# A post-norm transformer pair on one core: half 1's normed tiles turned one by one, the next batch's norm scales behind its scores, its normed tiles two per step

## The chip, the cores and the metric

The kernel runs on one core of a Trainium2 chip. The metric is the device time of one execution in microseconds; shown are three timed runs and one execution under the profiler. The engines are called TensorE (PE, with PEld for its weight loads), VectorE (DVE), ScalarE (ACT), GpSimd (POOL) and SyncE (SP).

## The reference

8192 tokens of width 256 (8 batches of 1024) go through two layers. Every sublayer adds its input and is normed afterwards. Cut to the part that the last stage computes:

```python
x = _layernorm(x + _L0_attn_ref(...))     # first stage
x = _layernorm(x + _L0_ffn_ref(...))      # experts: second stage; the norm: last stage
...
Q, K, V = X @ W_q + b_q, X @ W_k + b_k, X @ W_v + b_v
A = softmax(einsum('bsd,btd->bst', Q, K) / 16, axis=2)
x = _layernorm(x + einsum('bst,btv->bsv', A, V))
...
scores = sigmoid(xf @ gate.T)              # 8 experts, 2 groups of 4
# the two best of the better group, their scores divided by their sum
lat = xf @ fc1_w.T                         # 256 -> 128
he = relu2(xs @ w1[e].T) @ w2[e].T         # per expert, 128 -> 128
routed = comb @ fc2_w.T                    # 128 -> 256
shared = relu2(xf @ up_w.T) @ down_w.T     # 256 -> 1024 -> 256
x = _layernorm(x + routed + shared)
```

The norm is `(x - mean) / sqrt(var + 1e-5)` over the 256 channels of a token.

## The kernel before, in words

Three stages run one after the other: `stage_a` (first attention and routing), `stage_b` (the first layer's experts) and `stage_c` (everything from the norm in front of the second attention on). Only `stage_c` is touched. It takes one batch of 1024 tokens after the other, as 8 tiles of 128 tokens and, from the third norm on, in two halves of four tiles. Every float32 matrix is kept as a high and a low part, and `product` adds three products (high x high, high x low, low x high).

The order of the work stands in one table, `ORDER`, a list of units; each engine goes through the list and does its share of each unit. The engines meet only through semaphores, so an engine that waits in one unit holds back all its later units. ScalarE takes the batch's loop as a program of its own, with two units placed elsewhere. The units that matter here:

- `("norm3", h)` (L1702): ScalarE norms the four tiles of half `h` of `x2` (memory called `b_wout_raw` in the profile) into `x3` (`b_win_raw`). For half 0 the scales come from VectorE (`ln3`), for half 1 from GpSimd (`scale_second`).
- `("x3T", h)` (L2048 and on): TensorE transposes half `h` of `x3`, two chunks of 128 channels by four tiles, eight transposes (L2053) into two PSUM banks. ScalarE copies the banks as high parts (`c_x3T_hi`), VectorE subtracts for the low parts (`c_x3T_lo`, L1870).
- `("gate", h)`, `("gateT", h)`, `("scoreT", h)`: the router. `route` on VectorE is a chain of small steps; VectorE's copy into `c_scoreT` (L1924) is what SyncE stores and spreads over the partitions.
- `("up", (h, p))`: four products of the shared hidden layer. ScalarE takes the relu (L1738) and the square's high part (L1743), VectorE squares from PSUM (L1957) and so frees the bank, GpSimd subtracts for the low part (a "split", L1567, to `c_place`).
- `("expert", (h, p))`: four experts, each with a product of the latent in one of four PSUM banks and a share of the `down` products, which need the splits of the up units. VectorE multiplies with the scores (L1949) and squares (L1957), ScalarE copies the high part (L1746), GpSimd splits. The bank of expert product `k` is the one that up product `k`, or expert product `k` of the unit before, had: TensorE waits for VectorE's square of it.
- `("latent", h)`, `("comb", h)`, `("out", h)`: latent, combination of the experts, and the sum of everything. For `out`, VectorE adds two banks to `x3` (L1962) and takes four statistics (L1965).
- `("ln2", 0)`: VectorE turns the statistics of the *next* batch's input (`pre`, built up by the `combine` units) into scale and shift for all eight tiles, in the sixteen small steps of `norm_scale` (L148, L149, L150, and L97 through `Chain.then`), each waiting for the one before. `("ln3", 0)` and `("ln4", 0)` run the same sixteen steps on four tiles.
- `norm_x2(b + 1, t)` (L1641, L1630): ScalarE norms tile `t` of the next batch's `pre` into `x2`. It has no unit of its own, but is called inside the expert units: one tile behind each expert's copy, tiles 0 to 3 in `("expert", (0, 1))`, tiles 4 to 7 in `("expert", (1, 0))`. The unit `x2T` at the batch's end transposes them.

The last batch has neither `ln2`, `combine`, `norm_x2` nor `x2T`. The order of the units from half 0's last part on, before:

```python
("combine", 7), ("up", (0, 1)), ("ln2", 0), ("x3T", 1), ("expert", (0, 0)), ("gate", 1), ("expert", (0, 1)), ("gateT", 1),
("comb", 0), ("up", (1, 0)), ("scoreT", 1), ("out", 0), ("latent", 1), ("up", (1, 1)), ("ln4", 0), ("expert", (1, 0)),
("expert", (1, 1)), ("comb", 1), ("x2T", 0), ("x2T", 1), ("out", 1)]
```

Of the kernel before, what the change touches and what calls it, by code (L numbers as in the profile page):

```python
# [33 lines left out]
P = 128  # L34
# [28 lines left out]
def wait_past(eng, sem, value):  # L63

    if not isinstance(value, int) or value > 0:
        eng.wait_ge(sem, value)
# [1228 lines left out]
def stage_c(nc, d, weights, slots, gates, x2, x3_rows, pre, late, results_stored, wqk_raw, wqk_in):  # L1295
# [18 lines left out]
             ("gateT", 0), ("latent", 0), ("mix", 7), ("up", (0, 0)), ("scoreT", 0), ("combine", 6), ("norm3", 1),  # L1314
             ("combine", 7), ("up", (0, 1)), ("ln2", 0), ("x3T", 1), ("expert", (0, 0)), ("gate", 1), ("expert", (0, 1)), ("gateT", 1),
             ("comb", 0), ("up", (1, 0)), ("scoreT", 1), ("out", 0), ("latent", 1), ("up", (1, 1)), ("ln4", 0), ("expert", (1, 0)),
             ("expert", (1, 1)), ("comb", 1), ("x2T", 0), ("x2T", 1), ("out", 1)]
# [30 lines left out]
    with ExitStack() as ctx:  # L1348
# [279 lines left out]
        def _(act):  # L1628
# [12 lines left out]
            def norm_x2(b, t):  # L1641
                if is_first(b) and t % HTILES == 0:
                    act.wait_ge(pre_chain, (t // HTILES + 1) * (HTILES + NORM_STEPS))
                elif t == 0:
                    act.wait_ge(pre_chain, (b + 1) * PRE_STEPS + NORM_STEPS)
                    wait_past(act, x3_done, 2 * b)
                norm = normed(x2, pre, t, pre_scale, pre_shift)
                if t % HTILES == HTILES - 1:
                    norm.then_inc(x2_done, 1)
# [21 lines left out]
            def body(b, end):  # L1671
# [8 lines left out]
                for unit in units:  # L1680
# [16 lines left out]
                    elif kind == "norm3":  # L1697
# [6 lines left out]
                        for t in range(HTILES * j, HTILES * (j + 1)):  # L1704
                            last = normed(x3, x2, t, scale, shift)
                        last.then_inc(x3_done, 1)
                    elif kind == "x3T":
# [17 lines left out]
                    elif kind in ("up", "expert"):  # L1725

                        lag = 1 if kind == "up" else 0
                        for k in range(CHUNKS + lag):
# [18 lines left out]

                            if k < CHUNKS and unit in (("expert", (0, 1)), ("expert", (1, 0))) and not end:
                                norm_x2(b + 1, CHUNKS * j[0] + k)
                            elif k < CHUNKS and unit == ("expert", (1, 1)):  # L1750
                                norm4(b, k)
# [24 lines left out]
        def _(v):  # L1776
# [84 lines left out]
            def body(b, end):  # L1861
# [12 lines left out]
                for unit in order(b):  # L1874
# [83 lines left out]
                    elif kind == "out":  # L1958
                        for g in range(2):
                            at = HTILES * j + 2 * g  # L1960
                            v.wait_ge(v_full, n + g + 1)
                            v.tensor_tensor(x3[:, at:at + 2, :], ps[:, v_bank(unit, g), :].rearrange("p (t c) -> p t c", c=C), x3[:, at:at + 2, :], ALU.add).then_inc(v_free, 1)  # L1962
                        for t in range(HTILES):
                            v.wait_ge(v_free, n + t // 2 + 1)
                            v.bn_stats(stats[:, HTILES * j + t, :], x3[:, HTILES * j + t, :]).then_inc(stats_done, 1)  # L1965
                    elif kind == "ln4":
                        v.wait_ge(x3_done, 2 * b + 2)
                        scale_half(b, 2, 0)
# [33 lines left out]
        def _(pe):  # L2002
# [8 lines left out]
            def body(b, end):  # L2011
# [7 lines left out]
                for unit in order(b):  # L2019
# [28 lines left out]
                    elif kind == "x3T":  # L2048
                        pe.wait_ge(x3_done, 2 * b + j + 1)
                        for c in range(CH):  # L2050
                            out = v_open(pe, b, unit, c)
                            for t in range(HTILES):
                                last = pe.transpose(out[:, bass.ts(t, P)], x3[:, HTILES * j + t, bass.ts(c, P)], ident[:])  # L2053
                            last.then_inc(v_full, 1)
                    elif kind == "gate":
# [144 lines left out]
```

## Time and profile before

| what | us |
|---|---|
| timed runs | 1971.8, 1969.98, 1971.37 |
| their median | 1971.37 |
| the profiled execution | 1963.96 |
| its span | 1961.9 |
| mean granted clock of TensorE | 0.983 |

The span is the time between the first and the last instruction in the profile; the execution's own time is 2.1 us longer. The profiled execution is 0.4% below the median of the timed runs. `stage_c` takes the time from about 722 us on, and from its second batch on one batch follows the other every 151 us (the transposes of half 1 start at 973.64, 1124.98, 1276.20, 1427.42, 1578.35, 1729.42). Batch 1 is the one from which rows are shown. The timeline gives start, duration, engine, line, operation, what is written and read, and in brackets how long the engine was idle before and what released it; instructions of a kind that follow each other stand in one row with their count.

### The profile page before, as it was taken

Reading aid. Unit: us, or ns where it says so; the run is one execution under the profiler, and the core shown is the slowest. Engines: PE = TensorE matmul, PEld = TensorE weight load, DVE = VectorE, ACT = ScalarE, POOL = GpSimd, SP = SyncE. Lnnn points to the kernel's source line nnn. Section 1 sums busy time; section 2 is a strip of 40 time slices with the busy share of each in tenths; the row PEclk is TensorE's granted clock in tenths of the full one; section 3 lists DMA queues with packets and bytes.
Section 4 is the critical chain, followed back from the end, with each engine's and each line's share of the span. In section 5 each row is a group of like instructions: output and inputs, shape, how many; then the busy total and the mean of one; then the engine's idle time right before and its main releaser. Section 6 shows DMA issues by size and latency. Waiting matters only on the chain.

```text
span 1961.9 us, 35538 instructions
## 1 busy us (share of the span) xinstructions
PE 1860.4 (95%) x11756; PEld 1625.0 (83%) x11756; DVE 1354.9 (69%) x3205; ACT 870.6 (44%) x1623; POOL 861.5 (44%) x1165
## 2 busy tenths in 40 slices
PE   7999998599999989999999999999999999999996
PEld 6888887389999978788788788888878878878885
DVE  4788888644444565886886786876876886786664
ACT  4445554333333414444444445345454445444443
POOL 4267778531111142453454354354265265255054
PEclk9999999699999989999999999999999999999998
DMA  4111222323222331112212211221221112111011
GB/s 156 65 65 65 98 75 87 109 93 100 87 86 86 120 82 49 60 44 66 65 44 61 62 53 46 48 82 45 44 84 48 44 45 87 39 49 55 12 44 65
DMA packets 81639, 133.04 MB, mean 68 GB/s; under 512 B 11328, under 2 KB 62144, under 8 KB 81376
## 3 DMA queue, kind: packets, MB, share of 16 engines
q1 hardware_dynamic: 71984, 104.96, 16.0%
q0 software_dynamic: 9520, 26.36, 5.4%
q8 instruction: 75, 1.23, 0.3%
q14 instruction: 60, 0.49, 0.1%
HBM read 105.57 MB, written 25.72 MB: 67 GB/s over the span
## 4 chain that ended last, share of the span: by engine, by line
PE 62%; DVE 6%; issue 5%; POOL 3%; ACT 3%; DMA 1%; POOLq 0%; DVEq 0%; ACTq 0%
PE c_ps L118 10%; PE c_ps L120 10%; PE c_ps L119 10%; PE b_ps L118 5%; PE b_ps L119 5%; PE b_ps L120 5%; PE c_ps L133 3%; PE c_ps L134 3%; PE c_ps L135 3%; PE c_ps L2043 2%; PE c_ps L2104 2%; PE c_ps L2106 2%; PE c_ps L2105 2%; POOL c_pool_tmp L97 1%; ACT b_win_raw L1630 1%
## 5 line engine op out<-in xcount | busy, mean ns | idle before, releaser
L1567 POOL TENSOR_TENSOR c_place<-c_shared_place,c_place 128x512 fp32r<-128x512 f32 x256 | 324.8, 1293 | 197.4 <-ACT c_place L1746 114.3
L1558 POOL DMA_INDIRECT c_gathered<-expert_results,c_slots x112 | 112.2, 1002 | 324.4 <-DVE c_pre L1798 300.9
L1957 DVE SCALAR_TENSOR_TENSOR c_shared_place<-c_ps,c_shared_place 128x512 f32<-128x512 f32 x256 | 170.3, 683 | 54.4 <-ACT c_shared_place L1738 54.2
L118 PE MATMUL c_ps<-c_place 128*128 128x256 f32 (+1 forms) x520 | 149.2, 287 | 10.4 <-DVE c_place L1870 6.4
L1746 ACT ACTIVATE c_place<-c_shared_place 128x512 fp32r<-128x512 f32 x128 | 80.3, 630 | 174.0 <-DVE c_shared_place L1957 173.0
L133 PE MATMUL c_ps<-c_downT_hi,c_place 128*128 128x256 f32 x512 | 151.9, 297 | 2.4 <-POOL c_place L1567 2.4
L119 PE MATMUL c_ps<-c_place 128*128 128x256 f32 (+1 forms) x520 | 147.8, 284 | 0.0
L120 PE MATMUL c_ps<-c_place 128*128 128x256 f32 (+1 forms) x520 | 147.8, 284 | 0.0
L134 PE MATMUL c_ps<-c_downT_lo,c_place 128*128 128x256 f32 x512 | 145.1, 283 | 0.0
L1058 POOL DMA_INDIRECT b_xs<-x_rows,expert_tokens x56 | 57.9, 1033 | 198.3 <-PE b_ps L1246 175.8
L135 PE MATMUL c_ps<-c_downT_hi,c_place 128*128 128x256 f32 x512 | 144.8, 283 | 0.0
L1692 ACT ACTIVATE c_shared_place<-c_ps,c_shift_s 128x1024 f32<-128x1024 f32 x64 | 71.5, 1117 | 160.8 <-DVE c_shift_s L1893 160.2
L118 PE MATMUL b_ps<-b_wout_hi,b_hT_hi 128*128 128x256 f32 x448 | 127.2, 284 | 0.0
L120 PE MATMUL b_ps<-b_wout_hi,b_hT_lo 128*128 128x256 f32 x448 | 126.8, 283 | 0.0
L119 PE MATMUL b_ps<-b_wout_lo,b_hT_hi 128*128 128x256 f32 x448 | 126.7, 283 | 0.0
L118 PEld LDWEIGHTS c_ps<-c_place 128*128 128x128 f32 x520 | 100.4, 193 | 17.9 <-DVE c_place L1870 11.6
L1738 ACT ACTIVATE c_shared_place<-c_ps 128x512 f32<-128x512 f32 x128 | 75.4, 595 | 88.3 <-PE c_ps L120 64.1
L1199 DVE SCALAR_TENSOR_TENSOR b_hT_lo<-b_ps,b_hT_hi 128x512 fp32r<-128x512 f32 x112 | 76.1, 689 | 52.4 <-ACT b_hT_hi L1109 52.4
L118 PE MATMUL c_ps<-c_x3T_hi,c_upT_hi 128*128 128x512 f32 x256 | 100.4, 392 | 5.7 <-DVE c_shared_place L1957 5.7
L133 PEld LDWEIGHTS c_ps<-c_downT_hi,c_place 128*128 128x128 f32 x512 | 97.3, 190 | 9.4 <-POOL c_place L1567 5.4
L118 PE MATMUL c_ps<-c_x2T,c_place 128*128 128x512 f32 x256 | 104.2, 407 | 0.0
L1674 ACT ACTIVATE c_place<-c_ps 128x512 fp32r<-128x512 f32 x128 | 69.2, 594 | 77.2 <-PE c_ps L2043 77.2
(421 smaller groups left out, 6139.6 us busy)
## 6 DMA issues: line engine op xcount, KB each, us to landing
c_x2T<-score_rows SPq DMA_DIRECT2D x64, 512.0 KB, 5.4
b_win_raw<-xT SPq DMA_DIRECT2D x8, 1024.0 KB, 6.5
a_x_rows<-x SPq DMA_DIRECT2D x8, 1024.0 KB, 5.6
x_rows<-a_x SPq DMA_DIRECT2D x8, 1024.0 KB, 4.5
c_pre<-x_rows SPq DMA_DIRECT2D x8, 1024.0 KB, 5.6
out<-b_win_raw SPq DMA_DIRECT2D x16, 512.0 KB, 3.0
b_win_raw<-w_in SPq DMA_DIRECT2D x7, 1024.0 KB, 5.6
b_wout_raw<-w_out SPq DMA_DIRECT2D x7, 1024.0 KB, 6.0
```

Of the source, the lines that this page charges most:

```text
L118: pe.matmul(out, lh, rh, start=(j == 0), stop=False)
L119: pe.matmul(out, lh, rl, start=False, stop=False)
L120: last = pe.matmul(out, ll, rh, start=False, stop=(j == len(terms) - 1))
L133: pe.matmul(out, lh, rh, start=False, stop=False)
L134: pe.matmul(out, lh, rl, start=False, stop=False)
L135: last = pe.matmul(out, ll, rh, start=False, stop=(stop and j == len(terms) - 1))
L1199: v.scalar_tensor_tensor(hT_lo[:, h, k, :], ps[:, bank, :], 0.0, f32(hT_hi[:, h, k, :]), ALU.max, ALU.subtract).then_inc(bank_free, 1)
L1558: pool.indirect_dma_start(rows[:, a, :], None, d["ys"], bass.IndirectOffsetOnAxis(ap=slots[:, a, t:t + 1], axis=0), bounds_check=TRASH + P ...
L1567: pool.tensor_tensor(hid_lo[:, place, :], square[:, place % RING, :], f32(hid_hi[:, place, :]), ALU.subtract).then_inc(hid_split, 1)
L1738: act.activation(relu[:, place % RELU_RING, :], ps[:, s_bank(unit, k), :], ACT.Relu).then_inc(relu_up, 1)
L1746: act.activation(hid_hi[:, place, :], square[:, place % RING, :], ACT.Copy).then_inc(hid_hi_done, 1)
L1957: v.scalar_tensor_tensor(square[:, place % RING, :], ps[:, s_bank(unit, k - lag), :], 0.0, factor, ALU.max, ALU.mult).then_inc(s_free, 1)
```

## The change

It has three parts. (1) `norm3` on ScalarE signals `x3_done` after each tile and no longer once per half; TensorE's `x3T` goes tile by tile, waits for each tile, and turns both chunks of it before the next. The counts that others wait for are adapted (four times as many signals per half). (2) The unit `ln2` moves from its place in front of `("x3T", 1)` to behind `("scoreT", 1)`. (3) `norm_x2` for all eight tiles is called in `("expert", (1, 0))`, two tiles behind each expert's copy.

```diff
-             ("combine", 7), ("up", (0, 1)), ("ln2", 0), ("x3T", 1), ("expert", (0, 0)), ("gate", 1), ("expert", (0, 1)), ("gateT", 1),
-             ("comb", 0), ("up", (1, 0)), ("scoreT", 1), ("out", 0), ("latent", 1), ("up", (1, 1)), ("ln4", 0), ("expert", (1, 0)),
+             ("combine", 7), ("up", (0, 1)), ("x3T", 1), ("expert", (0, 0)), ("gate", 1), ("expert", (0, 1)), ("gateT", 1),
+             ("comb", 0), ("up", (1, 0)), ("scoreT", 1), ("ln2", 0), ("out", 0), ("latent", 1), ("up", (1, 1)), ("ln4", 0), ("expert", (1, 0)),
...
-                    wait_past(act, x3_done, 2 * b)
+                    wait_past(act, x3_done, TILES * b)
...
-                            last = normed(x3, x2, t, scale, shift)
-                        last.then_inc(x3_done, 1)
+                            normed(x3, x2, t, scale, shift).then_inc(x3_done, 1)
...
-                            if k < CHUNKS and unit in (("expert", (0, 1)), ("expert", (1, 0))) and not end:
-                                norm_x2(b + 1, CHUNKS * j[0] + k)
+                            if k < CHUNKS and unit == ("expert", (1, 0)) and not end:
+                                norm_x2(b + 1, 2 * k)
+                                norm_x2(b + 1, 2 * k + 1)
...
-                        v.wait_ge(x3_done, 2 * b + 2)
+                        v.wait_ge(x3_done, TILES * b + TILES)
...
-                        pe.wait_ge(x3_done, 2 * b + j + 1)
-                        for c in range(CH):
-                            out = v_open(pe, b, unit, c)
-                            for t in range(HTILES):
-                                last = pe.transpose(out[:, bass.ts(t, P)], x3[:, HTILES * j + t, bass.ts(c, P)], ident[:])
-                            last.then_inc(v_full, 1)
+                        outs = [v_open(pe, b, unit, c) for c in range(CH)]
+                        for t in range(HTILES):
+                            pe.wait_ge(x3_done, TILES * b + HTILES * j + t + 1)
+                            for c in range(CH):
+                                last = pe.transpose(outs[c][:, bass.ts(t, P)], x3[:, HTILES * j + t, bass.ts(c, P)], ident[:])
+                                if t == HTILES - 1:
+                                    last.then_inc(v_full, 1)
```

On VectorE, at the unit's old place between the squares of up (0, 1) and the low parts of half 1's transposes, before:

```order
L1957 SCALAR_TENSOR_TENSOR c_shared_place<-c_ps,c_shared_place 128x512 x4
L148 TENSOR_TENSOR c_tmp<-c_pre_stats 128x8
L149 TENSOR_TENSOR c_pre_shift<-c_pre_stats 128x8
L150 SCALAR_TENSOR_TENSOR c_tmp<-c_pre_stats 128x8
...
L97 SCALAR_TENSOR_TENSOR c_pre_scale<-c_tmp,c_pre_scale 128x8
L97 SCALAR_TENSOR_TENSOR c_pre_shift<-c_pre_shift,c_pre_scale 128x8
L1870 TENSOR_TENSOR c_x3T_lo<-c_ps,c_x3T_hi 128x512 x2
L1949 SCALAR_TENSOR_TENSOR c_shared_place<-c_ps,c_x2T 128x512 x2
```

In the changed program the low parts (L1870) follow the squares (L1957) at once, and the sixteen steps stand on the same engine behind the copy of half 1's scores:

```order
L1924 COPY c_scoreT<-c_ps 32x128
L148 TENSOR_TENSOR c_tmp<-c_pre_stats 128x8
L149 TENSOR_TENSOR c_pre_shift<-c_pre_stats 128x8
L150 SCALAR_TENSOR_TENSOR c_tmp<-c_pre_stats 128x8
...
L97 SCALAR_TENSOR_TENSOR c_pre_scale<-c_tmp,c_pre_scale 128x8
L97 SCALAR_TENSOR_TENSOR c_pre_shift<-c_pre_shift,c_pre_scale 128x8
L1962 TENSOR_TENSOR b_win_raw<-c_ps,b_win_raw 128x512 x2
L1965 BN_STATS c_stats<-b_win_raw 128x6 x4
L1870 TENSOR_TENSOR c_lat_lo<-c_ps,c_lat_hi 128x512
L1957 SCALAR_TENSOR_TENSOR c_shared_place<-c_ps,c_shared_place 128x512 x4
```

So the sums of half 0 (L1962), its statistics, the latent's low part and the four squares of up (1, 1) now stand behind the sixteen steps.

On TensorE, the transposes of half 1 with what they wait for (line 2053 is `x3T` in both), before and changed:

```order
L2053 MATMUL c_ps<-c_ident,b_win_raw 128x128 [waits c_v_free,c_x3_done]
L2053 MATMUL c_ps<-c_ident,b_win_raw 128x128 x3
L2053 MATMUL c_ps<-c_ident,b_win_raw 128x128 [waits c_v_free]
L2053 MATMUL c_ps<-c_ident,b_win_raw 128x128 x3
L118 MATMUL c_ps<-c_lat_hi,c_w1T_hi 128x512 [waits c_s_free,c_v_free]
```

```order
L2053 MATMUL c_ps<-c_ident,b_win_raw 128x128 [waits c_x3_done,c_v_free]
L2053 MATMUL c_ps<-c_ident,b_win_raw 128x128
L2053 MATMUL c_ps<-c_ident,b_win_raw 128x128 [waits c_x3_done]
L2053 MATMUL c_ps<-c_ident,b_win_raw 128x128
```

The pair with its wait stands four times, once per tile. The product behind it, the first of expert (0, 0), waits for its bank (`c_s_free`) and the latent's low part as before.

## Rows read from the trace of the kernel before

**Rows 1.** The page, part 1: busy time, share of the span, instructions.
```profile
PE 1860.4 (95%) x11756; PEld 1625.0 (83%) x11756; DVE 1354.9 (69%) x3205; ACT 870.6 (44%) x1623; POOL 861.5 (44%) x1165
```

**Rows 2.** Waits: engine, line <- waited for: us in all, times, longest.
```profile
PE c_ps L118 <- DVE c_shared_place L1957: 9.4, 21, 0.9
PE c_ps L2053 <- ACT b_win_raw L1630: 9.3, 7, 1.5
```

**Rows 3.** Timeline, TensorE, batch 1: start, us, instruction [idle before <-releaser].
```profile
973.64 1.09 PE L2053 MATMUL c_ps<-c_ident,b_win_raw 128*128 128x128 f32 x8 [1.50 <-ACT b_win_raw L1630]
974.93 0.47 PE L118 MATMUL c_ps<-c_lat_hi,c_w1T_hi 128*128 128x512 f32 x1 [0.20 <-DVE c_shared_place L1957]
...
976.46 0.39 PE L2093 MATMUL c_ps<-c_zeros 128*128 128x512 bf16 x1 [0.60 <-POOL c_place L1567]
...
981.46 0.39 PE L133 MATMUL c_ps<-c_downT_hi,c_place 128*128 128x256 f32 x1 [0.34 <-POOL c_place L1567]
...
986.31 0.40 PE L120 MATMUL c_ps<-c_x3T_hi,c_gateT_lo 128*8 128x512 f32 x1
987.02 0.47 PE L118 MATMUL c_ps<-c_lat_hi,c_w1T_hi 128*128 128x512 f32 x1 [0.32 <-DVE c_shared_place L1957]
```

**Rows 4.** Timeline, ScalarE, the same stretch.
```profile
971.51 2.07 ACT L1630 ACTIVATE b_win_raw<-b_wout_raw,c_shift,c_scale 128x256 f32<-128x256 f32 x4 [2.24 <-POOL c_shift L97]
973.49 1.05 ACT L1738 ACTIVATE c_shared_place<-c_ps 128x512 f32<-128x512 f32 x2
...
977.78 1.08 ACT L1674 ACTIVATE c_x3T_hi<-c_ps 128x512 fp32r<-128x512 f32 x2
...
997.99 0.17 ACT L1713 ACTIVATE c_expd<-c_ps 128x32 f32<-128x32 f32 x1
```

**Rows 5.** Timeline, VectorE, the same stretch.
```profile
974.10 1.29 DVE L1957 SCALAR_TENSOR_TENSOR c_shared_place<-c_ps,c_shared_place 128x512 f32<-128x512 f32 x2 [2.21 <-ACT c_shared_place L1738]
...
977.48 0.21 DVE L148 TENSOR_TENSOR c_tmp<-c_pre_stats 128x8 f32<-128x8 f32 x1
...
983.79 1.29 DVE L1870 TENSOR_TENSOR c_x3T_lo<-c_ps,c_x3T_hi 128x512 fp32r<-128x512 f32 x2
```

**Rows 6.** Timeline, GpSimd, batch 1: splits for half 0 and for up (1, 0).
```profile
971.43 9.97 POOL L1567 TENSOR_TENSOR c_place<-c_shared_place,c_place 128x512 fp32r<-128x512 f32 x8
...
1006.36 5.10 POOL L1567 TENSOR_TENSOR c_place<-c_shared_place,c_place 128x512 fp32r<-128x512 f32 x4 [7.17 <-DVE c_shared_place L1957]
```

**Rows 7.** Timeline, VectorE, from the sums `out` of half 0 on.
```profile
1009.16 1.27 DVE L1962 TENSOR_TENSOR b_win_raw<-c_ps,b_win_raw 128x512 f32<-128x512 f32 x2
...
1011.67 0.66 DVE L1870 TENSOR_TENSOR c_lat_lo<-c_ps,c_lat_hi 128x512 fp32r<-128x512 f32 x1
...
1017.34 1.27 DVE L148 TENSOR_TENSOR c_tmp<-c_stats 128x4 f32<-128x4 f32 x1
...
1022.48 1.29 DVE L1949 SCALAR_TENSOR_TENSOR c_shared_place<-c_ps,c_x2T 128x512 f32<-128x512 f32 x2
1023.69 0.68 DVE L1957 SCALAR_TENSOR_TENSOR c_shared_place<-c_ps,c_shared_place 128x512 f32<-128x512 f32 x1
```

**Rows 8.** Timeline, VectorE, `ln3` with GpSimd idle: first step, and what follows.
```profile
936.73 0.15 DVE L148 TENSOR_TENSOR c_tmp<-c_stats 128x4 f32<-128x4 f32 x1
...
939.55 1.22 DVE L1889 TENSOR_REDUCE c_neg_max<-c_ps 128x1 f32<-128x1024 f32 x1
```

**Rows 9.** Timeline, TensorE: first products of expert (1, 0) and (1, 1).
```profile
1015.82 0.39 PE L118 MATMUL c_ps<-c_lat_hi,c_w1T_hi 128*128 128x512 f32 x1
...
1024.57 0.41 PE L118 MATMUL c_ps<-c_lat_hi,c_w1T_hi 128*128 128x512 f32 x1
```

**Rows 10.** Windows: stretch: us, TensorE busy (x), granted clock, DMA share, GB/s.
```profile
1124.00:1136.60 12.60, 10.48 (x70) 1.00 0.41 145
...
1275.20:1287.80 12.60, 11.32 (x68) 0.86 0.38 152
...
1278.00:1279.00 1.00, 0.95 (x3) 0.50 0.99 377
```

## The prediction

> **What bounds the kernel now.** I read the page first: TensorE is busy 95% of the span [rows 1]. Work that is moved on another engine therefore counts only where TensorE waits for it. The list of waits shows how little that is in the last stage: 9.3 us for ScalarE's normed tiles and 9.4 us for VectorE's squares, in seven to twenty-one places [rows 2]. Then I took one batch (batch 1, 943 to 1042 us; the batches repeat every 151 us) engine by engine. What the reader is to see there: at the transposes of half 1 TensorE waits 1.50 us, then 0.20 us for VectorE, 0.60 and 0.34 us for GpSimd, then 0.3 us more for VectorE behind the gate product [rows 3], and from there to the next batch it hardly waits. That full stretch is where the sixteen steps of the norm scales (the unit `ln2`) are moved to.
>
> I count 0.2%, some 4 us, as what a measurement of this kernel can tell from no change.
>
> **Half 1's tiles turned one by one.** ScalarE norms four tiles from 971.51 to 973.58, at 0.5 us each, and the eight transposes start at 973.64 [rows 3, 4]. Turned one by one, six of them run earlier and the last two end near 973.9 and not 974.73. But the next product starts at 974.93 because it needs the PSUM bank that VectorE's first square frees (974.10 plus 0.69), and that square needs the relu that ScalarE starts at 973.49, behind the normed tiles [rows 3 to 5]. Nothing in this chain moves. The wait in front of the transposes turns into a longer wait behind them. Nor do copies of the transposes start earlier: ScalarE takes them after the up products' squares. I cost this part at 0; its cover is the relu, and if it were gone GpSimd's first four splits (971.43 plus four at 1.25 us [rows 6]) would still hold TensorE until 976.46. The three added waits on TensorE find their tiles ready in half 0 and fall into idle time in half 1.
>
> **`ln2` leaves its old place.** There the sixteen steps take VectorE from 977.48 to 983.79, 6.31 us [rows 5]. Without them the low part of half 1's transposes, and with it the squares of expert (0, 0), come about 5 us earlier: the copies of ScalarE end at 978.86 [rows 4], so the low parts are done near 979.6 and no longer at 985.0, and the squares follow. What is late next is GpSimd, and it is late already: the products at 976.46 and 981.46 wait for its splits, which run back to back from 971.43 [rows 3, 6], and the change doesn't touch these. So only the third wait goes: the first product of expert (0, 1) starts at 987.02 where it could have followed at 986.31 + 0.23 [rows 3]. **Gain: 0.5 us in each of seven batches** (the eighth has no `ln2`).
>
> **`ln2` in its new place.** VectorE now has it between the copy of half 1's scores and the sums `out` of half 0. All VectorE does for half 1 is queued behind it: the two sums and four statistics, the low part of the latent, the four squares of up (1, 1) and the scales of `ln4`. Two of these have TensorE waiting: the first product of expert (1, 0) needs the latent's low part and the bank that the first of the four squares frees.
> - VectorE comes to this place at 1009.16 [rows 7], with the 0.5 us gained 1008.66.
> - The length of the sixteen steps depends on GpSimd. With GpSimd quiet the same steps on half as many tiles take 2.83 us [rows 8]; `ln4` next to GpSimd's splits takes 5.14 us, its first step alone 1.27 us [rows 7], and `ln2` in its old place 6.31 us. There the last of the eight splits ends at 981.40, twelve steps follow in the 2.4 us until 983.79, 0.2 us each [rows 5, 6], and the first four took the 3.9 us before that: a step that meets a split waits for its end. In the new place the splits of up (1, 0) run until 1011.46 [rows 6], 0.5 us earlier after the change: 2.3 us of being held, with three steps done in it as in `ln4`, then thirteen free ones, 2.6 us. I take 4.9 us.
> - The sums start near 1013.6, the latent's low part 2.51 us later (1009.16 to 1011.67), the first square 0.6 us after that, at 1016.7; it ends at 1017.4, and TensorE follows 0.14 us behind, as at 974.93 [rows 3, 5]. TensorE has been ready since 1015.82 - 0.5 [rows 9]: **it waits 2.2 us, and stands 1.7 us later than before.**
> - The third relu needs the buffer and bank of the first square, so on ScalarE relu, square and relu (some 0.6 us each, as the relus of [rows 4]) follow from 1017.4, then one more square on VectorE, and VectorE comes to `ln4` near 1019.7, not 1017.34: 2.4 us late. `ln4` (5.1 us, since the splits are late too) and the squares up to the first freed bank (1.9 us, 1022.48 to 1024.37 [rows 7]) end near 1026.75. TensorE would be there at 1017.55 + 8.75 + 0.1 = 1026.4 [rows 9]: another 0.5 us of waiting. Before, this bank came only 0.2 us ahead of its use, so there is no slack to take up the delay.
>
> So each batch but the last is **2.3 us longer** at expert (1, 1), all gain counted in. From there to the next batch TensorE is full in both, and the other engines are late by the same amount as TensorE, so they meet it as before.
>
> For the steps' length the Trainium skill (SBUF — State Buffer, Who interferes with whom) has a rule: a VectorE instruction with two SBUF inputs contends with a GpSimd instruction that reads SBUF, and the loser is blocked for the whole of the other's instruction. The trace agrees for the steps named above. By that rule the hold ends with the last split, as I count it; by the plain row of the old place the steps would again take 6.31 us and the batch would be 3.7 us longer.
>
> **The next batch's normed tiles, two per step.** On ScalarE four tiles leave expert (0, 1), where TensorE waits for none, and expert (1, 0) has two per step. One step there is then a copy, some 0.6 us like the others of its size [rows 4], and two tiles of 0.5 us, 1.6 us against the 2.2 us (8.75 over four [rows 9]) that TensorE takes for a step, so ScalarE keeps up. Their reader, the transposes for the next batch, comes a whole expert unit and `comb` later. One side effect is good: ScalarE's exponential for the gate, held by copies and norms until 997.99 [rows 4], can start 1 us earlier, and the routing with it. But the squares behind it follow TensorE's products, so VectorE gains no more than the 0.5 us already counted. No DMA is added or moved: slots, rows and stores are issued behind `out` as before, and half 1's scores go out 0.5 us earlier. Cost 0.
>
> **Sum.** 7 x 2.3 = 16 us. The profiled execution took 1963.96 us (span 1961.9), so its like would be 1980; the timed runs, with their median of 1971.37, are what the forecast is for: **1987.4 us**. Bounds of the one unknown, the steps' length: 2.83 us (GpSimd quiet) brings expert (1, 0) 0.4 us earlier than before, and `ln4` is still 0.2 us late, in all +0.2 us per batch, 1973 us; 6.31 us gives 1014.97 for the sums, +3.7 us per batch, 1997 us. I take the value between because the end of the splits is a row and the hold follows it.
>
> **Rivals.**
> - *It fits (faster).* From 1008.66 to 1015.32 there are 6.66 us, and what must follow the steps takes 3.9 us. If the steps take 2.8 us or less and `ln4` is not late, only the gain remains: 1971.4 - 7 x 0.5 = 1968 us. Against it: the quiet row has 2.83 us, on half as many tiles, and here GpSimd works beside it [rows 6, 8]. Chance 0.08.
> - *Gain and loss even out.* GpSimd's splits, fed earlier, end before VectorE comes. The steps take 3 us: +0.2 to +0.4 us per batch, 1973 to 1974 us. Chance 0.09.
> - *The clock falls behind the new wait.* Once in the trace, after the cluster of waits at batch 3's transposes, the granted clock was 0.50 (1.2 GHz), 0.86 as the mean of the 12.6 us [rows 10], so 3.5 us at half rate; this cost nothing, since TensorE would have waited for GpSimd there. At the new place nothing hides it: 3.5 us at half rate lose 1.75 us per fall. In every batch: 7 x 1.75 = 12, so 2000 us; in two or three, about 1992. For it: the new wait of 2.2 us is longer than any other in the batches. Against: the same cluster of waits in the next earlier batch, 2.6 us in all, left the clock at 1.00 [rows 10]. Chance 0.11.
>
> The forecast keeps 0.72. The range, 1972 to 1998, holds the bounds and most of the clock's case. Faster 0.08, within 0.2% 0.09, slower 0.83.
>
> **What the new profile would show.** Transposes of half 1 in four pairs from 972.1 on and the product behind them still at the same distance from the relu; the wait of the first product of expert (0, 1) gone; the steps of `ln2` behind the scores' copy, 4.9 us long, the first ones ending with a split; a wait of about 2.2 us in front of expert (1, 0) and 0.5 us in front of expert (1, 1), both on VectorE's square; a batch of 153.5 us. I am wrong if the steps take under 3 us, if TensorE doesn't wait there, or if the product after the transposes starts earlier and GpSimd's splits with it.

## The result, and the profile after

| | us |
|---|---|
| changed kernel, median of 4 runs | 1991.21 (1990.76 to 1991.84) |
| kernel before on the same chip, median of 4 runs | 1970.81 (1969.98 to 1971.8) |
| ratio | 1.0103, interval 1.0091 to 1.0115 |
| the changed kernel's profiled execution | 1991.59 |
| its span, and mean granted clock | 1989.5, 0.979 |

The changed kernel is slower by 20.4 us. The profiled executions differ by 27.6 us, which is too much: the one of before started the first expert of `stage_c` at 823.86, the changed one at 830.32, though nothing ahead of `stage_c` was touched (of the eleven further kernels below seven are at 828.8 to 830.7 there, four, all on one other chip, at 824.0 to 827.5). So 6.5 us of the 27.6 come from outside the change, and 21.1 us from the last stage. One of the five timed executions of e2, below, took 3946 us, twice as long as all others, and is left out of its ratio. All below is of that stage, and positions are taken relative to the batch's first product of expert (0, 0).

The page, part 1, of the changed kernel (busy time, share of the span, instructions), to set beside [rows 1]:

```profile
PE 1870.6 (94%) x11756; PEld 1629.9 (82%) x11756; DVE 1352.7 (68%) x3205; ACT 869.3 (44%) x1623; POOL 865.6 (44%) x1165
```

Every engine has as many instructions as before. TensorE shows 10 us more busy time for the same work, part of which is time at the lower clock.

Its list of waits (engine, line <- waited for: us in all, times, longest), as [rows 2]:

```profile
PE c_ps L118 <- DVE c_shared_place L1957: 28.6, 26, 2.0
...
PEld c_ps L2053 <- ACT b_win_raw L1630: 5.7, 21, 0.3
```

The last line is of the transposes' weight loads (PEld), not of their matmuls. Its counterpart before is

```profile
PEld c_ps L2053 <- ACT b_win_raw L1630: 12.5, 8, 1.9
```

The matmuls' own row, 9.3 us before, is no longer in the list: they idle some 0.2 us per batch between the pairs. The weight loads' wait for normed tiles shrank from 12.5 to 5.7 us and fell apart into 21 of at most 0.3 us. The wait for VectorE's squares grew from 9.4 to 28.6 us, of which seven times 2.0 us are new and stand in front of expert (1, 0). It moved, and it grew.

Timeline of TensorE in the changed kernel, batch 1, as [rows 3, 9], and at the end the same two products of batch 5:

```profile
981.76 1.82 PE L2053 MATMUL c_ps<-c_ident,b_win_raw 128*128 128x128 f32 x8
984.44 0.47 PE L118 MATMUL c_ps<-c_lat_hi,c_w1T_hi 128*128 128x512 f32 x1 [0.86 <-DVE c_shared_place L1957]
...
985.98 0.39 PE L2094 MATMUL c_ps<-c_zeros 128*128 128x512 bf16 x1 [0.61 <-POOL c_place L1567]
...
990.96 0.39 PE L133 MATMUL c_ps<-c_downT_hi,c_place 128*128 128x256 f32 x1 [0.35 <-POOL c_place L1567]
...
996.03 0.39 PE L118 MATMUL c_ps<-c_lat_hi,c_w1T_hi 128*128 128x512 f32 x1
...
1026.90 0.47 PE L118 MATMUL c_ps<-c_lat_hi,c_w1T_hi 128*128 128x512 f32 x1 [2.02 <-DVE c_shared_place L1957]
...
1030.55 0.63 PE L118 MATMUL c_ps<-c_lat_hi,c_w1T_hi 128*128 128x512 f32 x1
...
1037.28 0.40 PE L118 MATMUL c_ps<-c_lat_hi,c_w1T_hi 128*128 128x512 f32 x1
...
1644.04 0.47 PE L118 MATMUL c_ps<-c_lat_hi,c_w1T_hi 128*128 128x512 f32 x1 [2.02 <-DVE c_shared_place L1957]
...
1653.59 0.47 PE L118 MATMUL c_ps<-c_lat_hi,c_w1T_hi 128*128 128x512 f32 x1 [0.60 <-DVE c_shared_place L1957]
```

The eight transposes now spread over 1.82 us, and the wait that stood ahead of them stands behind them (0.86). The waits for GpSimd's splits are there as before, 0.61 and 0.35. The wait at expert (0, 1), 996.03, is gone. At 1026.90 stands the new one, 2.02 us. In batch 1 the next product takes 0.63 us where such a one takes 0.40, and expert (1, 1) follows without a second wait (1037.28); in batch 5 the second wait is there, 0.60.

Windows (stretch: us, TensorE busy (x), granted clock, DMA share, GB/s), batch 1 behind the new wait, and batch 5 over the same place:

```profile
1028.00:1031.00 3.00, 3.00 (x15) 0.50 0.11 44
1640.00:1654.00 14.00, 11.38 (x72) 1.00 0.37 132
```

0.50 is the lower level, 1.2 GHz; batch 5 kept 2.4 GHz through.

ScalarE, batch 1, as [rows 4], and the pairs of the next batch's normed tiles:

```profile
981.01 2.08 ACT L1630 ACTIVATE b_win_raw<-b_wout_raw,c_shift,c_scale 128x256 f32<-128x256 f32 x4 [2.25 <-POOL c_shift L97]
983.00 1.06 ACT L1737 ACTIVATE c_shared_place<-c_ps 128x512 f32<-128x512 f32 x2
...
1006.00 0.18 ACT L1712 ACTIVATE c_expd<-c_ps 128x32 f32<-128x32 f32 x1
...
1036.31 0.63 ACT L1745 ACTIVATE c_place<-c_shared_place 128x512 fp32r<-128x512 f32 x1 [6.60 <-DVE c_shared_place L1957]
1036.84 1.08 ACT L1630 ACTIVATE b_wout_raw<-c_pre,c_pre_shift,c_pre_scale 128x256 f32<-128x256 f32 x2
1037.83 0.61 ACT L1745 ACTIVATE c_place<-c_shared_place 128x512 fp32r<-128x512 f32 x1
```

VectorE, batch 1, as [rows 5, 7]:

```profile
983.61 1.29 DVE L1957 SCALAR_TENSOR_TENSOR c_shared_place<-c_ps,c_shared_place 128x512 f32<-128x512 f32 x2 [2.22 <-ACT c_shared_place L1737]
...
987.91 1.29 DVE L1870 TENSOR_TENSOR c_x3T_lo<-c_ps,c_x3T_hi 128x512 fp32r<-128x512 f32 x2 [0.84 <-ACT c_x3T_hi L1674]
...
1018.06 1.08 DVE L148 TENSOR_TENSOR c_tmp<-c_pre_stats 128x8 f32<-128x8 f32 x1
1019.07 0.16 DVE L149 TENSOR_TENSOR c_pre_shift<-c_pre_stats 128x8 f32<-128x8 f32 x1
1019.15 1.26 DVE L150 SCALAR_TENSOR_TENSOR c_tmp<-c_pre_stats 128x8 f32<-128x8 f32 x1
1020.44 0.17 DVE L97 SCALAR_TENSOR_TENSOR c_tmp<-c_tmp 128x8 f32<-128x8 f32 x1
...
1022.97 1.29 DVE L1962 TENSOR_TENSOR b_win_raw<-c_ps,b_win_raw 128x512 f32<-128x512 f32 x2
...
1025.49 0.67 DVE L1870 TENSOR_TENSOR c_lat_lo<-c_ps,c_lat_hi 128x512 fp32r<-128x512 f32 x1
1026.08 1.28 DVE L1957 SCALAR_TENSOR_TENSOR c_shared_place<-c_ps,c_shared_place 128x512 f32<-128x512 f32 x2
...
1029.31 0.17 DVE L148 TENSOR_TENSOR c_tmp<-c_stats 128x4 f32<-128x4 f32 x1
...
1034.38 1.29 DVE L1949 SCALAR_TENSOR_TENSOR c_shared_place<-c_ps,c_x2T 128x512 f32<-128x512 f32 x2
```

GpSimd, batch 1, as [rows 6]:

```profile
980.94 9.97 POOL L1567 TENSOR_TENSOR c_place<-c_shared_place,c_place 128x512 fp32r<-128x512 f32 x8
...
1015.10 5.28 POOL L1567 TENSOR_TENSOR c_place<-c_shared_place,c_place 128x512 fp32r<-128x512 f32 x4 [6.98 <-ACT c_place L1742]
```

The sixteen steps run from 1018.06 to 1022.97: 4.91 us. The first and the third step took 1.08 and 1.26 us, and they end at 1019.14 and 1020.41, 0.03 us behind the ends of the third and the fourth of the splits that run one after the other from 1015.10 to 1020.38. From 1020.44 on the steps come every 0.2 us. Then the sums, the latent's low part at 1025.49, and the square that frees the bank at 1026.08; TensorE follows at 1026.90. `ln4` starts at 1029.31, 44.87 us after the batch's start, where it was 42.41 [rows 7]. Early in the batch VectorE and ScalarE are ahead of where they were: the transposes' low parts start 3.47 us after the batch's first product and not 8.86 (987.91, and [rows 5]), the exponential 21.56 and not 23.06 (1006.00, and [rows 4]). ScalarE's pairs of tiles come every 1.51 us, faster than TensorE's 2.1 us per step.

### The profile page after: what moved, and what is told of

It is laid out like the page before. It is cut to its first block, busy times and chain, and to the rows that moved or that the text cites. A ratio compares the mean times of both kernels' runs of the same rounds, so it can differ in the third digit from the quotient of the medians.

```text
span 1989.5 us, 35538 instructions
## 1 busy us (share of the span) xinstructions
PE 1870.6 (94%) x11756; PEld 1629.9 (82%) x11756; DVE 1352.7 (68%) x3205; ACT 869.3 (44%) x1623; POOL 865.6 (44%) x1165
## 4 chain that ended last, share of the span: by engine, by line
PE 59%; DVE 8%; issue 6%; POOL 4%; ACT 2%; DMA 1%; POOLq 0%; DVEq 0%; ACTq 0%
PE c_ps L118 9%; PE c_ps L120 9%; PE c_ps L119 9%; PE b_ps L118 5%; PE b_ps L120 5%; PE b_ps L119 5%; PE c_ps L133 3%; PE c_ps L135 3%; PE c_ps L134 3%; PE c_ps L2043 2%; POOL c_place L1567 2%; PE c_ps L2105 2%; PE c_ps L2107 1%; PE c_ps L2106 1%; POOL c_pool_tmp L97 1%
## 5 line engine op out<-in xcount | busy, mean ns | idle before, releaser
L1957 DVE SCALAR_TENSOR_TENSOR c_shared_place<-c_ps,c_shared_place 128x512 f32<-128x512 f32 x256 | 170.3, 684 | 49.2 <-ACT c_shared_place L1737 49.0
L133 PE MATMUL c_ps<-c_downT_hi,c_place 128*128 128x256 f32 x512 | 153.8, 300 | 2.1 <-POOL c_place L1567 2.1
L135 PE MATMUL c_ps<-c_downT_hi,c_place 128*128 128x256 f32 x512 | 146.9, 287 | 0.0
L1949 DVE SCALAR_TENSOR_TENSOR c_shared_place<-c_ps,c_x2T 128x512 f32<-128x512 f32 x128 | 86.7, 687 | 52.8 <-PE c_ps L120 42.1
```

Source lines behind the costliest of these rows:

```text
L133: pe.matmul(out, lh, rh, start=False, stop=False)
L135: last = pe.matmul(out, ll, rh, start=False, stop=(stop and j == len(terms) - 1))
L1949: v.scalar_tensor_tensor(square[:, place % RING, :], ps[:, s_bank(unit, k), :], 0.0, score_rows[:, bass.ts(e, HALF)], ALU.max, ALU.mult).t ...
L1957: v.scalar_tensor_tensor(square[:, place % RING, :], ps[:, s_bank(unit, k - lag), :], 0.0, factor, ALU.max, ALU.mult).then_inc(s_free, 1)
```

## The experiments

The kernels ran on three chips: the kernel before had 1970.77 us beside the first four (1970.81 beside the changed kernel), 1965.11 beside the next four, and 1970.68 beside the last three. So ratios and differences to the kernel before are compared, not times. Times are medians; a ratio comes from all executions and can differ from the quotient of two medians in its fourth digit. "Falls" are counted in the profiled execution: batches (of the seven with a next batch) in which the granted clock over the 12 to 13 us behind the place is 0.86 or 0.87 and not 1.00.

### e1_ln2_back: the unit back in its old place, the two other parts kept

```diff
-             ("combine", 7), ("up", (0, 1)), ("x3T", 1), ...
-             ... ("scoreT", 1), ("ln2", 0), ("out", 0), ...
+             ("combine", 7), ("up", (0, 1)), ("ln2", 0), ("x3T", 1), ...
+             ... ("scoreT", 1), ("out", 0), ...
```

> The changed kernel with the unit ln2 back in front of the transposes of half 1; the tile-by-tile transposes and the two normed tiles per step stay. Theory (all of the loss and all of the gain come from the sixteen steps' place): as the kernel before, 1970.8 us within 0.2%, no wait in front of expert (1, 0), the wait of 0.3 us behind the gate product back. Rival (the two normed tiles per step or the added waits on TensorE cost too): more than 1975 us.

Measured: 1970.49 us, ratio 0.9998 (0.9989 to 1.0007). Its wait for the squares:

```profile
PE c_ps L118 <- DVE c_shared_place L1957: 13.0, 18, 0.9
```

None of these is at expert (1, 0) or (1, 1). **The whole loss hangs on the place of `ln2`**, within the 1.8 us of the interval. But the profile also shows four falls of the clock behind the transposes, where the profile of before has one. They cost little here: each takes the place of the wait at expert (0, 1), two leave the batch as it was at expert (1, 0), and the other two make it 0.4 us longer there; in e4 below, where that wait is gone, a fall costs 0.5 to 0.9 us.

### e2_half_turned: the changed kernel with four tiles turned together

```diff
-                        for t in range(HTILES):
-                            pe.wait_ge(x3_done, TILES * b + HTILES * j + t + 1)
-                            for c in range(CH):
+                        pe.wait_ge(x3_done, TILES * b + HTILES * j + HTILES)
+                        for c in range(CH):
+                            for t in range(HTILES):
```

> The changed kernel with the transposes of half 1 as before (they wait for all four normed tiles). Theory (turning tile by tile is worth nothing, since the product behind is released by VectorE's square): 1991.2 us within 0.2%, the wait in front of the transposes 1.5 us and behind them 0.2 us again. Rival A (turning tile by tile saved 0.7 us per batch): 1996 us. Rival B (it costs, by waking the clock gate more often): 1988 us.

Measured: 1988.88 us, ratio 1.0087 (1.0071 to 1.0102). TensorE at the transposes of batch 3:

```profile
1290.93 1.09 PE L2053 MATMUL c_ps<-c_ident,b_win_raw 128*128 128x128 f32 x8 [1.46 <-ACT b_win_raw L1630]
1292.22 0.47 PE L118 MATMUL c_ps<-c_lat_hi,c_w1T_hi 128*128 128x512 f32 x1 [0.20 <-DVE c_shared_place L1957]
```

The waits of [rows 3] are back, and the product behind the transposes stands where it stood; no fall there in seven batches, two behind the new wait. It is 2.3 us faster than the changed kernel (four executions each, the slowest here 1989.61, the fastest there 1990.76), with intervals of the ratios that overlap: a hint that turning the tiles one by one costs something, by the clock.

### e3_behind_out: the steps one unit later, behind the sums of half 0

```diff
-             ... ("scoreT", 1), ("ln2", 0), ("out", 0), ("latent", 1), ...
+             ... ("scoreT", 1), ("out", 0), ("ln2", 0), ("latent", 1), ...
```

> The changed kernel with ln2 one unit later, behind the sums and statistics of half 0, in front of the latent's low part. The same work stands in front of the first square of up (1, 1). Theory (two of the five us of the steps are being held by GpSimd's splits): the steps now start 2.5 us later, at the end of the splits, and take 2.9 us; TensorE waits under 0.2 us in front of expert (1, 0) and some 0.6 us in front of expert (1, 1); 1972 to 1974 us. Rival (the steps' own number and the queue behind them count, not the hold): no change against the changed kernel, 1991 us.

Measured: 1976.35 us, ratio 1.0024 (1.0014 to 1.0034). VectorE, batch 1:

```profile
1014.69 1.27 DVE L1962 TENSOR_TENSOR b_win_raw<-c_ps,b_win_raw 128x512 f32<-128x512 f32 x2
1015.89 1.38 DVE L1965 BATCH_NORM_STATS2 c_stats<-b_win_raw 128x6 f32<-128x256 f32 x4
1017.20 0.14 DVE L148 TENSOR_TENSOR c_tmp<-c_pre_stats 128x8 f32<-128x8 f32 x1
...
1020.06 0.69 DVE L1870 TENSOR_TENSOR c_lat_lo<-c_ps,c_lat_hi 128x512 fp32r<-128x512 f32 x1
```

The sums and statistics, which read PSUM or have one input in SBUF, keep their length (1.27 and 1.38 us) beside GpSimd's splits, and then the steps meet none: 2.86 us for the same sixteen steps. TensorE doesn't wait at expert (1, 0), and 0.56 to 0.59 us at expert (1, 1), as `ln4` is still late. So **2 of the 4.9 us were the hold by GpSimd, and taking them away took 15 us off the loss** (the falls behind the new wait went with them). The Trainium skill (SBUF — State Buffer, Who interferes with whom) says that a VectorE instruction with two SBUF inputs contends with a GpSimd instruction that reads SBUF, and one with at most one such input, outside some faster modes, doesn't. The trace agrees: the steps took 1.08 and 1.26 us beside splits and 0.14 to 0.17 us without, the sums 1.29 and 1.27 us. I had forecast 1972 to 1974, the second wait included, and it is 5.6 us above before: not in the forecast were the two batches with a fall behind the transposes, 0.9 us each.

### e4_behind_expert: the steps behind expert (0, 0), where VectorE idles

```diff
-             ... ("x3T", 1), ("expert", (0, 0)), ("gate", 1), ...
+             ... ("x3T", 1), ("expert", (0, 0)), ("ln2", 0), ("gate", 1), ...
```

(and `ln2` taken out behind `("scoreT", 1)`)

> The changed kernel with ln2 between expert (0, 0) and the gate product's copy, where VectorE now idles 0.9 and 1.7 us and is several us ahead of what TensorE needs. Theory: the steps take 4 to 5 us there (held by two splits) but delay nothing that TensorE waits for; the gain of 0.5 us in each of seven batches is left: 1967 us. Rival (the delay reaches the routing and with it the low part of comb, which TensorE needs for out of half 0): 1971 us or more, with a new wait in front of out.

Measured: 1969.27 us, ratio 0.9991 (0.9982 to 1.0). VectorE, batch 2:

```profile
1143.34 0.16 DVE L148 TENSOR_TENSOR c_tmp<-c_pre_stats 128x8 f32<-128x8 f32 x1
1143.42 0.17 DVE L149 TENSOR_TENSOR c_pre_shift<-c_pre_stats 128x8 f32<-128x8 f32 x1
1143.51 0.16 DVE L150 SCALAR_TENSOR_TENSOR c_tmp<-c_pre_stats 128x8 f32<-128x8 f32 x1
1143.70 1.18 DVE L97 SCALAR_TENSOR_TENSOR c_tmp<-c_tmp 128x8 f32<-128x8 f32 x1
1144.92 1.22 DVE L97 TENSOR_TENSOR c_tmp<-c_tmp 128x8 f32<-128x8 f32 x1
...
1148.30 0.68 DVE L1918 COPY c_logit<-c_ps 8x512 f32<-8x512 f32 x1
```

The steps take 4.96 us here, since the fourth and fifth meet splits, and nobody waits for them. No wait is left at expert (0, 1), (1, 0) or (1, 1): a batch without a fall takes 150.3 to 150.9 us and not 150.9 to 151.3. Three batches have a fall behind the transposes and are up to 0.9 us longer, which gives back what the place saves.

### e5_no_steps: fifteen of the sixteen steps left out

This kernel leaves out all of `ln2` but its first step, so that the next batch's normed tiles are made with scales that are never computed; the time is that of all other work in the changed order.

```diff
-                norm_scale(v, chain, pre_stats[:], pre_scale[:], pre_shift[:], tmp[:])
+                chain.wait()
+                v.tensor_tensor(tmp[:, 0, :], pre_stats[:, :, 1], pre_stats[:, :, 4], ALU.subtract).then_inc(pre_chain, NORM_STEPS)
```

> The changed kernel with fifteen of ln2's sixteen steps left out (one VectorE step stays, so the next batch is normed with scales that are not its own). Theory (the steps' time at this place is the whole loss): no wait in front of expert (1, 0) or (1, 1), 0.5 us gained in each of seven batches less what clock falls behind the transposes cost, 1967 to 1970 us. Rival (something else in the changed kernel, such as two normed tiles per step, holds up expert (1, 0)): waits of some tenths of a us stay in front of expert (1, 0) or (1, 1), 1973 us or more.

Measured: 1961.89 us, ratio 0.9983 (0.9974 to 0.9992), 3.2 us below before, and no wait at expert (1, 0) or (1, 1). It is not the wait on the scores or the moved order that costs, but the steps' own time. Two falls behind the transposes are in this time.

### e6_kept_busy: eight multiplications with zeros in the new wait

```diff
+                        if j == (1, 0) and not end:
+                            pe.wait_ge(v_free, v_upto(b, ("scoreT", 1)))
+                            keep_busy(pe, ps[:, v_bank(("scoreT", 1)), :], zeros, 8)
```

> The changed kernel with eight multiplications of zeros on TensorE (some 1.7 us, into the bank of the scores' transposes, free by then) in front of expert (1, 0), where TensorE waits 2.0 us for VectorE. Theory (the wait itself is VectorE's, and in three of seven batches the clock falls behind it and costs another 1 us each): the granted clock stays at 1.00 in expert (1, 0), the wait shrinks to 0.3 us, expert (1, 0) starts at the same time; 1986 to 1989 us against 1991. Rival (the fall comes from the cluster of short waits over the whole batch, not from this wait): the falls stay, 1991 us.

Measured: 1983.23 us, ratio 1.0092 (1.0076 to 1.0107): 18.1 us above before, where the changed kernel is 20.4 above. TensorE, batch 1, the zeros and the first product of expert (1, 0):

```profile
1019.97 1.90 PE L127 MATMUL c_ps<-c_zeros 128*128 128x512 bf16 x8
1022.14 0.47 PE L118 MATMUL c_ps<-c_lat_hi,c_w1T_hi 128*128 128x512 f32 x1 [0.27 <-DVE c_shared_place L1957]
```

The wait is filled to 0.27 us, the product comes no earlier, the second wait is back in all seven batches (0.53 to 0.60) and no batch falls there; one falls behind the transposes. The same wait unfilled had falls behind it in three of seven batches of the changed kernel and in two of seven of e2. So the falls most likely are the clock's answer to that wait; with one profile of e6 chance isn't ruled out. They are worth about 2 us of the loss; the intervals overlap.

### e7_expert_half and e8_ln2_only: what the other parts give in the good place

e7 is e4 with the four tiles turned together (the edits of e4 and e2). e8 is the kernel before with nothing but `ln2` moved behind `("expert", (0, 0))`.

> ln2 between expert (0, 0) and the gate's copy, and the transposes of half 1 all after the fourth normed tile, as before; two normed tiles per step stay. Theory (turning tile by tile makes the clock fall behind the transposes more often: 11 of 28 batches with it against 1 of 14 without, at 0.9 us each where VectorE's wait is gone): hardly any fall, 1966 to 1968 us, 2 to 3 us under the same kernel with tiles turned one by one (1969.3). Rival (the counts are chance): 1969 us.

> The kernel before with ln2 alone moved, between expert (0, 0) and the gate's copy; transposes and normed tiles stay as they were before (four tiles in expert (0, 1)). Theory: as the run with the two per step, 1966 to 1968 us; ScalarE waits for the scales in expert (0, 1) no longer than it does anyway. Rival (ScalarE held in expert (0, 1) delays the high parts, GpSimd's splits and comb): 1970 us or more.

Measured: e7 1961.33 us, ratio 0.9984 (0.9974 to 0.9993); e8 1961.82 us, ratio 0.9981 (0.9972 to 0.9991). One fall each. The batches are alike (150.3 to 151.0 us, one of 151.3 in e7). Two normed tiles per step therefore give and cost nothing with `ln2` in this place: in e8 they come one per step. In the changed place of `ln2` this part was not taken away by itself.

### e9_tiles_again, e10_half_again, e11_tiles_busy: do the tiles one by one cost clock?

On one chip: e9 is e4 again, e10 is e7 again, and e11 is e9 with four multiplications with zeros between the transposes and expert (0, 0):

```diff
+                        if j == (0, 0) and not end:
+                            keep_busy(pe, v_open(pe, b, ("out", 0), 0), zeros, 4)
```

> The kernel of e4_behind_expert once more (ln2 behind expert (0, 0), transposes tile by tile), now on the same chip as its twin with the transposes of all four tiles together. Theory (tile by tile, the clock falls behind the transposes in about a third of the batches, 0.9 us each): two to three falls in the profile, 1 to 3 us slower than e10. Rival (the counts so far are chance): equal to e10 within 0.5 us.

> The kernel of e7_expert_half once more, same chip as e9 and e11: none or one fall in the profile; 0.2% under the kernel before.

> The kernel of e9 with four multiplications of zeros on TensorE (0.9 us) between the transposes of half 1 and the first product of expert (0, 0), in the 0.86 us that it waits there for VectorE. Theory (the falls come from the idle time there): none or one fall, the wait near 0.1 us, as e10 or up to 0.3 us slower per batch where the multiplications outlast the wait. Rival: two or three falls stay.

| | us | ratio to before | falls behind the transposes |
|---|---|---|---|
| e9, one by one | 1969.16 | 0.9989 (0.998 to 0.9998) | 3 of 7 |
| e10, four together | 1966.60 | 0.998 (0.997 to 0.999) | 1 of 7 |
| e11, one by one, zeros behind | 1966.85 | 0.9977 (0.9968 to 0.9986) | 0 of 7 |

Windows of 13 us that begin 3 us ahead of batch 2's first product of expert (0, 0), of e9, e10 and e11 in this order (stretch: us, TensorE busy (x), granted clock, DMA share, GB/s):

```profile
1128.29:1141.29 13.00, 11.36 (x63) 0.87 0.40 163
```

```profile
1128.20:1141.20 13.00, 10.35 (x69) 1.00 0.46 159
```

```profile
1127.88:1140.88 13.00, 11.85 (x74) 1.00 0.41 163
```

Timeline of TensorE in e11 at this place:

```profile
1128.19 1.83 PE L2053 MATMUL c_ps<-c_ident,b_win_raw 128*128 128x128 f32 x8
1129.86 1.03 PE L127 MATMUL c_ps<-c_zeros 128*128 128x512 bf16 x4
1130.88 0.47 PE L118 MATMUL c_ps<-c_lat_hi,c_w1T_hi 128*128 128x512 f32 x1
...
1132.41 0.39 PE L2096 MATMUL c_ps<-c_zeros 128*128 128x512 bf16 x1 [0.60 <-POOL c_place L1567]
```

The zeros fill the 0.86 us behind the transposes; the next product stands no earlier, the wait for the split behind it (0.60) is as it was, and the clock holds. Over all profiles, kernels that turn the tiles one by one fell behind the transposes in 17 of 49 batches (2, 4, 2, 3, 2, 1, 3 of seven), kernels that turn four together in 4 of 35 (1, 0, 1, 1, 1), e11 in none. The counts are of one execution per kernel. e9 over e10 is 2.6 us and e11 under e9 2.3 us by the medians, and the intervals of the ratios overlap. But the three ran on one chip, and every timed execution has its mean granted clock on record:

| | executions | mean us | mean granted clock |
|---|---|---|---|
| e9, one by one | 11 | 1969.0 | 0.9811 |
| e10, four together | 9 | 1967.1 | 0.9827 |
| e11, one by one, zeros behind | 11 | 1967.0 | 0.9831 |

The standard errors are 0.2 to 0.4 us and 0.0003 to 0.0004. A fall takes the mean over 13 us from 1.00 to 0.87, which is 0.0009 over the whole execution. So e9 has about two falls more per execution than e10 and e11, as the profiles have, and it is 1.9 and 2.1 us slower, four standard errors each. **Yes: in this place of `ln2` the tiles one by one cost 2 us, by the clock.**

## Why the prediction was right, and where it was not

The forecast was 1987.4 us and slower; it is 1991.21 us. Against before the loss is 20.4 us and not 16. That the time lies in the range says less, since the range reached from 1 to 27 us of loss; what speaks for the prediction is that each wait stands where it had it, with its length.

**Tiles one by one, cost 0: the chain held, the cost did not.** The relu (983.00), the square (983.61) and the product (984.44) keep their distances to each other, as the prediction had it. What it didn't price is the shape of the idle time: ahead of the change 1.50 us of waiting, a solid run of transposes and 0.20; after it pauses between the pairs (up to 0.3 us in the weight loads, 0.1 in the matmuls), then 0.86, 0.61 and 0.35. The clock fell behind that in 17 of 49 batches against 4 of 35. It is worth about 2 us for all batches with `ln2` behind expert (0, 0) (e9 against e10, and e11 brings them back); e2 against the changed kernel, 2.3 us with four executions each, agrees.

**`ln2` leaves: gain 0.5 us per batch: right.** Expert (0, 1) follows 11.59 us after the batch's start and not 12.09. GpSimd's splits bound expert (0, 0) in both.

**`ln2` in its new place: right in each step, to 0.2 us.** Steps 4.91 us (4.9 forecast), the wait at expert (1, 0) 2.02 us (2.2), the position there 1.57 us later (1.7). Where the clock holds, the second wait is 0.56 to 0.60 us (0.5) and the position at expert (1, 1) is 2.40 and 2.18 us later in batches 4 and 5 (2.3). e1 and e5 show that, with the falls behind it, this is all of the loss to within 2 us, e3 that the 2 us of hold by GpSimd make most of it.

**Two per step, cost 0: right** (e7 beside e8).

**The rival of the clock came true in part, at another price.** Its time for two or three falls, about 1992 us, is the nearest of all to the measured one, but partly by luck: its price per fall was too high, and it left out the falls behind the transposes. The clock fell behind the new wait in three of seven batches, not in none as the forecast had it, and the price of 1.75 us was too high: a fall delays TensorE until VectorE is there, so it takes the place of the second wait. Batches 0, 1 and 6 are 2.97, 3.20 and 3.01 us later at expert (1, 1), 0.7 to 0.9 above the 2.3. With the falls behind the transposes (batch 2: 3.27; batch 3: 2.92, where before had a fall too, which covered its wait at expert (0, 1), so that the 0.5 gain is missing) the sum in the profile is 7 x 2.3 = 16.1, plus 0.7, 0.9, 1.0, 0.6 and 0.7, 20.0 us. The last 1.1 us of the 21.1 arise behind expert (1, 1), nearly all in batches 4 and 5 (0.46 us each): there the kernel before had waited only 0.94 us for the normed tiles of the next batch and not 1.5. In those next batches, 5 and 6 of before, GpSimd's own norm scales for half 1 took 5.15 us from their first step to their last; in its batches 0 to 4 and in batches 0 to 6 of the changed kernel they took 5.66 to 5.68 us. ScalarE's tiles wait for them. Why they come out at one or the other is open. The prediction counts one fall in the trace of before. That holds for the place behind the transposes; the same trace has seven other stretches at 0.50, most of them ahead of the last stage.

So **the term that was mis-sized is the clock's**: the sum carried it at 0, it is 4 us in the last stage's profile, and the change raises it at two places, not at one.

Not tried: part 3 with the tiles where they were and part 2 kept. The normed tiles in expert (0, 1) would wait for scales that VectorE makes only behind the routing, which itself waits for an exponential that ScalarE has behind those tiles, so by the order of the programs neither engine could go on.

**The best version** is neither kernel: `ln2` behind `("expert", (0, 0))`, four tiles turned together, 0.2% under the kernel before on two chips (e7, e10, and e8 with one normed tile per step). e11 is as fast.

## What to carry to other kernels

Place small chained steps by two questions: who is queued behind them on their engine, and what does GpSimd do meanwhile; the same sixteen steps took 2.86 or 4.9 us for that reason, and cost 20 us, 6 us or nothing by their place. Before a wait is cut into pieces ("the tiles one by one"), ask whether anything behind it moves; here nothing did, and the pieces cost 2 us of clock. Where a fall of the clock replaces a wait that comes next, count the difference, not the fall.

## What the hardware showed unexpectedly

- The granted clock fell behind a single wait of 2.02 us in batches 0, 1 and 6 and not in 2 to 5, with the same wait in each. In batches 2 and 3 a fall behind the transposes had come earlier, in 4 and 5 none. Filling that wait to 0.27 us with multiplications by zeros left 0 of 7 (e6, one profile).
- At the transposes less idle time gave more falls: pairs with small gaps and 0.86 us behind them fell in 17 of 49 batches, one wait of about 1.5 us and a solid run in 4 of 35. Filling only the 0.86 us left 0 of 7 in e11's profile, and its eleven timed executions have the clock of e10 (0.9831 and 0.9827), not that of e9 (0.9811).
- The first three of the sixteen steps, which don't wait for each other, unlike the rest, start 0.08 us apart when nothing holds them (1143.34, 1143.42, 1143.51), the chained ones 0.20 us. Which of them a split of GpSimd held depended on when it came: the first and third in the changed kernel, the fourth and fifth in e4, 1.1 to 1.3 us each. The splits themselves kept their length: 1.29 to 1.31 us each beside these steps, 1.29 to 1.30 us before, where none stood beside them.
